# Another order of work between the last attention unit and the first expert batches

## The reference, cut to what matters

```
h = layernorm(x) * (1 + ca) + sa
x = x + ga * attention(h, W_K, W_Q, W_V, W_O)          # causal, 16 heads, d_head 128
h = layernorm(x) * (1 + cb) + sb
x = x + gb * ffn(h)

# ffn, L = 128, hidden sizes HID = [128, 256, 384, 512, 128, 256, 384, 512]
hd = h @ down_w + down_b
probs = softmax(h @ router_w + router_b - 1e-7 * cost)
topv, topi = top_k(probs, 2);  gate = softmax(topv)
out = sum over k, e of gate[k] * (gelu(gelu(hd * (topi[k] == e)) @ w1[e] + b1[e]) @ w2[e] + b2[e])
out = out + 0.1 * (gelu(gelu(hd) @ shared_w1 + shared_b1) @ shared_w2 + shared_b2)
out = out @ up_w + up_b + (gelu(h) @ core_w + core_b)
```

## Time and profile before

| | |
|---|---|
| median of 3 runs | 813.04 us (811.65 to 814.38) |
| profiled execution, its own time | 812.05 us |
| its span, first to last instruction | 810.0 us |
| busy: PE, DVE, ACT, POOL | 784.7, 679.5, 628.4, 441.2 us |
| mean granted TensorE clock | 0.996 |

### The profile page before, as it was taken

The page is one execution under the profiler, slowest core; times in us unless marked ns, Lnnn a source line. Parts: engine busy times, 40 slices in busy tenths (PEclk is TensorE's granted clock), DMA queues, the critical chain, the costliest instruction groups (busy, mean ns, idle before and its releaser), DMA issues.

```text
span 810.0 us, 14461 instructions
## 1 busy us (share of the span) xinstructions
PE 784.7 (97%) x4806; PEld 700.6 (86%) x4806; DVE 679.5 (84%) x1649; ACT 628.4 (78%) x1417; POOL 441.2 (54%) x305
## 2 busy tenths in 40 slices
PE   7899899999999999999999999999999989989997
PEld 6789898999999999999999999999999767778786
DVE  4789998888888888888888888889898989887967
ACT  3787878877887788877778888877778968876974
POOL 2555365654456655445566544576545474577654
PEclk9999999999999999999999999999999999999999
DMA  7262233343222444322344332244332230111231
GB/s 264 64 171 68 63 90 93 91 104 86 66 66 66 101 108 108 83 66 66 72 104 106 91 92 66 66 97 115 94 76 60 64 105 34 67 58 66 69 102 53
DMA packets 47593, 70.54 MB, mean 87 GB/s; under 512 B 5536, under 2 KB 38464, under 8 KB 47392
## 3 DMA queue, kind: packets, MB, share of 16 engines
q1 hardware_dynamic: 47008, 68.81, 32.4%
q0 software_dynamic: 368, 0.81, 0.3%
q10 hardware_dynamic: 144, 0.00, 0.0%
HBM read 25.49 MB, written 2.17 MB: 34 GB/s over the span
## 4 chain that ended last, share of the span: by engine, by line
PE 64%; ACT 17%; DVE 11%; issue 5%; POOL 2%; DMA 1%; SPq 0%; DVEq 0%; POOLq 0%
PE M L732 10%; PE M L733 9%; PE M L731 9%; PE T L731 7%; PE T L733 7%; PE T L732 7%; PE S L731 5%; PE S L733 5%; PE S L732 5%; ACT PB L623 4%; ACT PB L672 3%; ACT pth L699 2%; DVE S L1135 2%; ACT qk L685 2%; ACT hh L665 1%
## 5 line engine op out<-in xcount | busy, mean ns | idle before, releaser
L623 ACT ACTIVATE PB<-S,nb 128x128 f32<-128x128 f32 (+3 forms) x256 | 133.9, 533 | 109.9 <-DVE nb L1135 109.9
L580 POOL TENSOR_TENSOR ptl<-ptl,pth 128x640 fp32r<-128x640 f32 x126 | 196.8, 1584 | 31.9 <-ACT pth L699 31.9
L573 POOL TENSOR_TENSOR X<-X,fb 128x512 f32<-128x512 f32 x64 | 83.1, 1299 | 239.5 <-DVE fb L1172 239.5
L672 ACT ACTIVATE PB<-PB,ri 128x256 f32<-128x256 f32 (+3 forms) x256 | 124.5, 580 | 6.4 <-DVE ri L1144 6.3
L1135 DVE CUSTOM_DVE_ANT_0 S<-S,cc 128x128 f32<-128x128 f32 (+3 forms) x256 | 117.6, 523 | 1.3 <-PE S L733 1.3
L1124 DVE TENSOR_TENSOR qk<-M,qk 128x512 fp32r<-128x512 f32 x108 | 74.6, 691 | 45.0 <-ACT qk L685 45.0
L1151 DVE STREAM_TRANSPOSE gab<-PB 128x256 f32<-128x256 f32 (+2 forms) x192 | 109.4, 623 | 0.0
L731 PE MATMUL S<-qk 128*128 128x128 f32 (+3 forms) x256 | 86.6, 338 | 4.6 <-DVE qk L1124 4.6
L699 ACT CAST pth<-ptl 128x640 fp32r<-128x640 f32 x128 | 87.8, 745 | 1.1 <-DMA ptl<-gab 1.1
L731 PE MATMUL M<-hh,W 128*128 128x512 f32 x222 | 86.7, 390 | 0.5 <-DVE hl L1110 0.5
L732 PE MATMUL M<-hl,W 128*128 128x512 f32 x222 | 86.5, 390 | 0.0
(11 more groups left out here) (255 smaller groups left out, 2410.7 us busy)
## 6 DMA issues: line engine op xcount, KB each, us to landing
ptl<-gab SPq DMA_DIRECT2D x256, 160.0 KB, 3.0
stage<-in_wat SPq DMA_DIRECT2D x16, 512.0 KB, 5.0
gab<-scw SPq DMA_DIRECT2D x16, 256.0 KB, 3.2
tmp<-scw SPq DMA_DIRECT2D x16, 256.0 KB, 3.6
X<-in_x SPq DMA_DIRECT2D x3, 512.0 KB, 8.3
stage<-in_wfa SPq DMA_DIRECT2D x3, 512.0 KB, 4.5
out<-X SPq DMA_DIRECT2D x3, 512.0 KB, 2.7
X<-in_wmod SPq DMA_DIRECT2D x1, 1024.0 KB, 11.8
```

The costliest lines, as they stand in the source:

```text
L573: pool.tensor_tensor(X[:, a:a + 512], X[:, a:a + 512], fb[:, c2 * 512:c2 * 512 + 512], ALU.add).then_inc(s_y, 1)
L580: pool.tensor_tensor(ptl[u % 2][:, s], ptl[u % 2][:, s].bitcast(F32), pth[u % 2][:, s].bitcast(F32), ALU.subtract).then_inc(s_pl, 1)
L623: ins = act.activation(PB[:, P_OFF[i]:P_OFF[i] + w], PS[bk][:, a:a + w], ACT.Exp, bias=nb[:, i:i + 1], scale=-1.0, accum_out=sm[:, i:i + 1])
L672: act.activation(p, p, ACT.Copy, scale=ri[:, i:i + 1]).then_inc(s_P3, 1)
```

## The change

Numbers in three tables are altered; no instruction is added or taken away. At the end of attention, `pt` of unit 62 goes ahead of `r` of sample 0, and router steps 6 to 9 go behind the first expert batch. Among the first batches of sample 0, router steps 10 to 12 go one batch later, steps 13 and 14 two batches later, the 512-wide weight piece goes behind `r` of sample 1, and the second half of the norm of sample 2 goes ahead of `dn` 1. At the end of sample 1, router steps 10 to 12 of sample 2 go from batch 17 to 18 and steps 13 and 14 from 18 to 19.

```diff
--- before.py
+++ after.py
@@ -104,8 +104,8 @@
         plan += [ev for group in steps for ev in group]
         plan += post.get(i, [])
     u = NU - 1
-    plan += [("S", u), ("wo", u // 2 - 2, 1), ("v", u // 2, 1), ("ex", u), ("ri", u), ("r", 0), ("rs", 0, 1),
-             ("rs", 0, 2), ("pt", u - 1), ("ra",), ("wx", u // 2 - 2, 1), ("b1",)] + [("rs", 0, k) for k in range(3, 10)] + [
+    plan += [("S", u), ("wo", u // 2 - 2, 1), ("v", u // 2, 1), ("ex", u), ("ri", u), ("pt", u - 1), ("r", 0),
+             ("rs", 0, 1), ("rs", 0, 2), ("ra",), ("wx", u // 2 - 2, 1), ("b1",)] + [("rs", 0, k) for k in range(3, 6)] + [
              ("dn", 0), ("z", u - 2)]
     return plan + [("norm", u), ("ty", u), ("tr", u), ("z", u - 1), ("ld", 22)]
 
@@ -129,17 +129,17 @@
             put(rest[0], j, ("rs", b, k))
         put(*weights, ("wt", b))
 
-    put(0, 0, ("rs", 0, 10), ("rs", 0, 11), ("rs", 0, 12))
-    put(0, 1, ("wo", last - 1, 0), ("rs", 0, 13), ("rs", 0, 14))
+    put(0, 0, ("rs", 0, 6), ("rs", 0, 7), ("rs", 0, 8), ("rs", 0, 9))
+    put(0, 1, ("wo", last - 1, 0), ("rs", 0, 10), ("rs", 0, 11), ("rs", 0, 12))
     put(0, 2, ("wo", last - 1, 1), ("wh", 21))
-    put(0, 3, ("pt", NU - 1))
-    put(0, 4, ("wx", last - 1, 1), ("wh", 22))
+    put(0, 3, ("pt", NU - 1), ("rs", 0, 13), ("rs", 0, 14))
+    put(0, 4, ("wx", last - 1, 1))
     put(0, 6, ("wt", 0), ("wl", 0), ("wl", 1), ("wl", 2), ("d0", 0))
     put(0, 7, ("z", NU - 1), ("st", 6, 0), ("st", 6, 1), ("d0", 1))
     put(0, 8, ("wo", last, 0), ("st", 6, 2), ("st", 6, 3), ("d0", 2))
     put(0, 9, ("wo", last, 1), ("wl", 3), ("nb", 6))
     put(0, 10, ("nm", 6, 0))
-    put(0, 11, ("dn", 1), ("nm", 6, 1))
+    put(0, 11, ("nm", 6, 1), ("dn", 1))
     put(0, 12, ("h2", 2, 0))
     put(0, 14, ("h2", 2, 1), ("st", 7, 0))
     put(0, 15, ("st", 7, 1), ("st", 7, 2))
@@ -149,13 +149,14 @@
     put(0, 19, ("nm", 7, 1))
     put(0, 20, ("dt",))
     router(1, ((0, 5), (0, 6), (0, (11, 11, 11, 12, 12, 14, 14, 15, 15, 15, 16, 16))), (0, 19))
+    put(0, 5, ("wh", 22))
     put(1, 1, ("h2", 3, 0))
     put(1, 3, ("D", 1))
     put(1, 4, ("h2", 3, 1))
     put(1, 5, ("D", 0), ("hs", 0, 0))
     put(1, 7, ("gx", 0, 0), ("hs", 0, 1))
     put(1, 9, ("gx", 0, 1))
-    router(2, ((1, 6), (1, 8), (1, (14, 14, 14, 15, 15, 16, 16, 17, 17, 17, 18, 18))), (2, 0))
+    router(2, ((1, 6), (1, 8), (1, (14, 14, 14, 15, 15, 16, 16, 18, 18, 18, 19, 19))), (2, 0))
     router(3, ((2, 4), (2, 5), (2, (11, 11, 11, 12, 12, 14, 14, 15, 15, 15, 16, 16))), (2, 19))
     for t in range(1, B):
         first = t == 1
```

## The result

The changed kernel took 816.77 us (median of 8 runs, 814.01 to 818.57), the kernel before beside it 813.0 us (8 runs, 811.01 to 816.45): ratio 1.0038, 95% interval [1.0021, 1.0056]. Run again under another label it took 818.21 us, ratio 1.0048 [1.003, 1.0065]. The forecast was 816.7. The profiled execution of the changed kernel took 816.57 us with a span of 814.5 and a mean granted clock of 0.989 (before: 812.05, 810.0, 0.996).

What follows compares the result with a forecast made beforehand. VectorE was taken to bound the end of attention; delays of 1.52 + 1.39 + 0.8 = 3.7 us, passed on whole with 0 from the later parts, gave 813.04 + 3.7 = 816.7 us, range 812.5 to 819.5.

Steps and rivals of the forecast that it cites:

- The bound: End of attention, 629.73 to 654.82: VectorE, busy 24.37 of 25.09 us, bounds the stretch and moves the end of `zt`.
- Part 1, `ur`: Subtraction ahead of the router: ScalarE's exp comes 2.0 us later, so the first `ur` goes from 634.55 to 636.07, 1.52 later.
- Part 1, steps 6 to 9: Router steps 6 to 9, 1.39 us that before filled VectorE's time ahead of `ur`, are still to be done after it.
- Part 2, the meetings: First batches: VectorE instructions started under GpSimd's lose 3.6 us in sum against 2.8 before, 0.8 more.
- The reading as each instruction's own time: Alternative for the meetings: the long rows carry over unchanged, and the delay stays at the 2.9 us of the first part.
- Sum at `wo`: The `wo` product that stood at 655.60 comes 1.52 + 1.39 + 0.8 = 3.7 us late.
- Part 3: Norm of sample 2 ahead of two gelus: 0, since ScalarE is full; bound for a gain 1.0 us.
- Part 4: Third batch's router steps later: TensorE's 2.1 us wait moves from `ur` to L912; 0, bound for a gain 2.1.
- sign of error: For the third and fourth parts: distance from the `wo` product to the end of the span shrinks by over 0.5 us.
- rival (b): TensorE's clock falls to 1.2 GHz behind its wait for the first L912, costing up to 1.7 us: 818.4; chance 0.15.

Runs made afterwards that it cites:

- e4: Changed kernel with only the subtraction of unit 62 put back behind router step 2; `wo` at 29.08, ratio to the kernel before 1.0023 [1.0006, 1.0039].
- e5: Changed kernel with router steps 13 and 14 of sample 0 moved behind the fourth and fifth batch's low parts; `wo` at 29.78, ratio to before 1.0047.
- e11: e5 with the transposes of the first sample's weights (L913) and what hangs on them also behind `z` of unit 63; `wo` at 26.34, ratio to before 1.003.
- e1: Kernel before with only the subtraction of unit 62 moved ahead of the router's r; `wo` at 28.19, ratio to before 1.0017.
- e13: Kernel before with sample 0's router steps 6 to 9 behind the first expert batch, 10 to 12 joined to 13 and 14; `wo` at 28.18, ratio 1.0032.
- e2: Kernel before with only the second half of the norm of sample 2 ahead of `dn` 1; `wo` at 25.94, ratio to before 1.0011.
- e3: Kernel before with only router steps 10 to 14 of sample 2 later, as in the change; `wo` at 25.92, ratio to before 1.0015.
- e7: Kernel before with the change's router order for sample 2 and its weight transposes (L912) one expert batch later; median 812.72 us, ratio to before 0.9973.
- e10: Changed kernel with the transposes of the third batch's weights (L913) one expert batch later; median 815.68 us, ratio to before 1.0019.
- e8: Kernel before with router steps 13 and 14 of sample 0 directly behind step 12, ahead of GpSimd's addition; median 812.87 us, ratio to before 0.9982.
- e9: Kernel before with the edits of e7 and e8 together; median 812.19 us against 814.29, ratio to before 0.9975.

## Why the prediction was right, step by step

**The bound.** Half right. VectorE is the chain that ends at `zt` in before, and it explains the changed kernel's time there. From the first cast to `zt`, 25.19 us became 29.03: 1.46 for the later `ur`, 1.4 for steps 6 to 9 (640.32 to 641.73), 0.8 for the meetings, 3.7 of 3.84. But "whatever it does there moves the end of `zt`" was too simple. e4, e5 and e11 show TensorE's chain through L913 and `z` beside it, in the changed kernel equal to the last tenth of a microsecond. That it did not end later there, and my sum was not changed by it, is luck: the stretch at half clock behind L913 lasted 3.4 us in both profiles of the changed kernel, and where it lasted 6.8, in e4, `zt` waited 1.34 for it. A sum for taking back only one of the parts would have been wrong, and in the expectations of e4 and e5 it was, by 1.3 to 2.1, by the estimate above because of the clock.

**Part 1, `ur`.** 1.52 forecast, 1.46 measured, 1.48 in e1. The exp was forecast 2.0 later and was 1.9 later behind the cast. (The row of the second gelu gives its end as 634.04, not 634.14 as the text says; the sum uses the former.)

**Part 1, steps 6 to 9.** 1.39 forecast, 1.4 in the changed kernel. e13 splits it: when `ur` is not held by the exp, taking them away brings 0.65 back at once, and 0.7 is left.

**Part 2, the meetings.** 3.6 forecast, 3.6 measured. Each is at its forecast place, but that the sum is hit to the tenth is luck, as misses of 0.2 to 0.4 cancel: clear 1.1 (1.3), wide piece 0.6 (0.2), step 13 0.8 (1.0), the next 1.1 (1.1), 512-wide piece 0 (0). The instruction that pays last is L1013, not the chained L1015 that I named. The reading as each instruction's own time, by which the sum stays at 2.9, is refuted by L1013 taking 1.30 and, moved in e5, 0.18. The three rows of before do not all end "just behind" GpSimd's, as the text says: the wide piece ends at 647.35 and the first half of L580 at 646.28. L913 went to 651.91, "later than 650".

**Sum at `wo`:** 3.7 forecast, 3.86 measured.

**Part 3:** 0 forecast, nothing at `ur` and `wo` in e2, at most 0.4 gained behind them.

**Part 4:** 0 forecast for the order itself, and that is what e3 and e4 have (154.4 and 154.1 us from `wo` to the end). In the changed kernel's own executions it was 155.8. The text gave as a sign of error that this distance shrinks by over 0.5; it grew by 1.4 instead, through rival (b), the clock, which I had placed at the wrong one of the two waits: behind the first L913 the half-clock stretch ties with VectorE and costs nothing that shows at `wo`, behind the second it costs 1.3 to 1.7 (by e7 and e10, and by e4). The stretch of the earlier trace rows lasts 3.4 us, from 697.6 to 701.05, and not the 4 of the text.

**Why the median still fits.** Between the two profiled executions the distance from cast to end grew by 5.2, not 3.7. The profile of before is a favourable one: in e1, e2, e8 and e13, whose order at the third batch is before's, TensorE waits 3.0 to 3.1 us for `ur` L1283 (2.1 in the earlier trace rows), has no half-clock stretch at 697 to 701 as in the earlier trace rows, and has one right behind that wait, and `wo` to end is 155.4 to 155.8. So the kernel before pays for such a stretch too, in some executions, and its median is 1 to 2.6 us over its profiled execution. How often it does I can't tell from one profile. The stretch that before does have, in the earlier trace rows, costs nothing that shows: e3 has none at all, and it takes 154.4 from `wo` to the end as well. The changed kernel's excess of 3.1 us by the ratio (3.9 in the second set) is then the 3.86 at `wo` and little else, which is what the forecast said. That the median came within 0.1 of 816.7 is luck: the medians of the kernel before lie between 813.0 and 814.7, and either set of the changed kernel has an interval of over 2.5 us.

## What to carry to other kernels

Ahead of a table load and two gelus on a full ScalarE, the two tiny instructions that release it are worth more than the long one that looks urgent; move the long one only if nobody queues behind the short ones. Count the overlaps of VectorE's instructions on SBUF with those of GpSimd one by one: a step of 0.19 us took up to 1.57, and moving such steps to a stretch in which GpSimd is idle gave 1.5 us here. Do not count a gain on VectorE before you know how long the product beside it takes at half clock. Where a wait ends several chains, ask of each waiting product what stands behind it on its engine, and measure from a landmark inside the kernel, since one execution's total can be a microsecond or two off its median.

## What the runs showed of the hardware that I had not expected

TensorE's granted clock stands at 0.50 for pieces of 3.4 us (in e4 and e13 two in a row, 6.8). Of those between 629 and 680 and between 720 and 740 each stands behind or around a wait of TensorE: 2.5 us for `ur`, 1.9 for L975 (e1), 2.2 to 3.6 for L913, 3.0 to 3.1 for `ur` and `G4l`. The other way round it does not hold: before had 1.9 for L975 and 2.1 for `ur`, e1 2.5 for its first `ur`, e3 2.8 for L912, e4 2.8 for its second L913 and e5 2.5 for its first `ur`, and their clock stayed at 1.00 there; so did it in these two spans behind all waits of 1.6 and less. A long wait is not needed either. Between 697 and 706 the profile of before, both of the changed kernel, e5 and e11 have one more stretch each, within 1.5 us behind the router's sixteen products of 16 columns, with no wait of over 0.3 us ahead of it; the other nine profiles have the same products there and no stretch. So a long wait makes a stretch likely and does not decide it. What does is open.

The spread of a kernel's runs goes with this clock. Over the 29 to 35 runs of the kernel before in each group, time and mean granted clock go together with r = -0.89 to -0.92 and 0.53 to 0.59 us for each 0.001 of clock. One stretch of 3.4 us at half is 0.0021 of the mean, so about 1.2 us, of the 1.7 us by which it holds up TensorE's work. Between kernels it shows as well: the mean clock over all runs was 0.9923 for before, 0.9870 for the changed kernel's second set and e5, 0.9891 for e10 and 0.9934 for e9. From the changed kernel to e10 it rose by the worth of one stretch. That a lower mean clock is the cause of a longer time, and not only found with it, is shown here for one stretch alone, the one behind the third batch's L913; for the one behind the first L913 it is the estimate given with e11.
